# Moving one projection tile, eight transposes and one gate past each other in the rounds of the first attention

## The reference

```python
q, k, v, s = hidden @ Wq, hidden @ Wk, hidden @ Wv, clip(hidden @ Ws, -32, 32)   # per head
z = cumlogsumexp(s, axis=time)
g = exp(concat([z[:1], z[:-1]]) - z);  p = exp(s - z)
hk_t = hk_{t-1} * g_t + k_t (x) p_t;   ok_t = q_t . hk_t         # first pass
pv = softmax(ok)                                                  # over the 64 slots
hv_t = hv_{t-1} * g_t + p_t (x) v_t;   ov_t = pv_t . hv_t        # second pass
o = ov * rsqrt(mean(ov^2) + 1e-5) * g_norm_weight * silu(hidden @ Wg)
x = layernorm(x + o @ Wo)
```

## Time and profile before

| | |
|---|---|
| median of 3 runs | 1235.19 us (1234.74 to 1239.53) |
| profiled execution | 1234.43 us; its span in the trace 1232.5 us |
| PE busy | 949.3 us, 77% of the span |
| DVE busy | 816.3 us, 66% |
| ACT busy | 485.0 us, 39% |
| POOL busy | 385.9 us, 31% |
| mean granted TensorE clock | 0.886 |

### The profile page before, as it was taken

The page is one execution under the profiler, slowest core; times in us unless marked ns, Lnnn a source line. Parts: engine busy times, 40 slices in busy tenths (PEclk is TensorE's granted clock), DMA queues, the critical chain, the costliest instruction groups (busy, mean ns, idle before and its releaser), DMA issues.

```text
span 1232.5 us, 18141 instructions
## 1 busy us (share of the span) xinstructions
PE 949.3 (77%) x5415; PEld 599.4 (49%) x5415; DVE 816.3 (66%) x1474; ACT 485.0 (39%) x823; POOL 385.9 (31%) x325
## 2 busy tenths in 40 slices
PE   6699999999999997448988888830694785888565
PEld 2356556565656555336655556500374443444333
DVE  6568778786878778785544333366677997465766
ACT  3534444534434443302323223204213443777164
POOL 0136472736556464302433333177001000000000
PEclk9699999999999998669999999965697756998787
DMA  4812112111112110220887787733101000000001
GB/s 151 310 56 88 51 55 64 60 55 51 55 52 89 51 43 1 91 71 18 250 254 241 238 260 233 209 95 96 62 1 69 1 1 1 1 0 1 1 1 35
DMA packets 54931, 106.64 MB, mean 87 GB/s; under 512 B 7433, under 2 KB 27537, under 8 KB 54385
## 3 DMA queue, kind: packets, MB, share of 16 engines
q1 hardware_dynamic: 49329, 90.99, 23.1%
q0 software_dynamic: 5568, 15.21, 4.3%
HBM read 86.61 MB, written 19.56 MB: 86 GB/s over the span
## 4 chain that ended last, share of the span: by engine, by line
PE 37%; DVE 27%; SPq 13%; issue 11%; ACT 5%; POOL 4%; DMA 3%; DVEq 0%; ACTq 0%; POOLq 0%
PE ps L617 6%; SPq L519 6%; PE ps L701 3%; PE ps L582 3%; PE ps L572 3%; PE ps L962 3%; DVE row_max L2003 2%; SPq L516 2%; SPq L525 2%; POOL yg L1184 2%; SPq L522 2%; PE ps L630 2%; DVE state L1544 2%; PE ps L1005 1%; PE ps L977 1%
## 5 line engine op out<-in xcount | busy, mean ns | idle before, releaser
L1128 POOL TENSOR_TENSOR state<-state,c_row 128x1024 f32<-128x1024 f32 x32 | 77.4, 2418 | 200.7 <-DVE state L1544 118.1
L617 PE MATMUL ps<-w_vg,xT 128*128 128x512 f32 x256 | 118.0, 604 | 10.2 <-DVE th L1568 10.2
L800 PE MATMUL ps<-w_gv,xgT 128*128 128x352 f32 x272 | 94.5, 480 | 25.3 <-DMA w_gv<-in_w_gv 23.9
L1121 POOL TENSOR_TENSOR drive<-du,b_row 128x1024 f32<-128x1024 f32 x32 | 89.5, 2797 | 55.9 <-DVE y L1694 55.9
L1555 DVE TENSOR_TENSOR aT<-ps,tri 128x768 f32<-128x768 f32 x64 | 59.2, 954 | 42.1 <-PE ps L582 42.1
L572 PE MATMUL ps<-xT,w_qks 128*128 128x512 f32 x192 | 85.0, 593 | 0.3 <-DMA w_qks<-in_wqks 0.3
L1544 DVE TENSOR_TENSOR_SCAN state<-decay,drive 128x1024 f32<-128x1024 f32 x32 | 83.5, 2611 | 0.0
L1168 POOL DMA_INDIRECT xg<-x_dram,tok_cur x68 | 66.6, 979 | 53.6 <-POOL tok_cur L1165 38.6
L2003 DVE TENSOR_REDUCE row_max<-ps 128x1024 f32 x64 | 74.2, 1217 | 7.4 <-PE ps L977 6.6
L617 PEld LDWEIGHTS ps<-w_vg,xT 128*128 128x128 f32 x256 | 46.6, 192 | 65.0 <-issue 45.7
L1801 DVE SCALAR_TENSOR_TENSOR g_th<-g_th,ps 128x176 f32<-128x176 f32 x76 | 25.6, 337 | 78.4 <-ACT g_th L1213 78.3
(11 more groups left out here) (284 smaller groups left out, 2115.3 us busy)
## 6 DMA issues: line engine op xcount, KB each, us to landing
w_gv<-in_w_gv SPq DMA_DIRECT2D x68, 352.0 KB, 4.1
w_dn<-in_w_dn SPq DMA_DIRECT2D x68, 176.0 KB
y_dram<-y_out SPq DMA_DIRECT2D x68, 128.0 KB, 3.5
b_row<-x_dbl_dram SPq DMA_DIRECT2D x16, 512.0 KB, 3.6
c_row<-x_dbl_dram SPq DMA_DIRECT2D x16, 512.0 KB, 4.7
y_dram<-blank SPq DMA_DIRECT2D x2, 3584.0 KB, 22.5
w_vg<-in_wvg SPq DMA_DIRECT2D x8, 512.0 KB, 3.3
w_qks<-in_wqks SPq DMA_DIRECT2D x8, 384.0 KB, 3.0
```

What stands on the lines that cost most here:

```text
L617: last = mm(bank(PJ + t % 2), xT[:, k, t * P:(t + 1) * P], w_vg[:, k, :], start=(k == 0), stop=(k == KD - 1))
L800: last = mm(ps[:, 2 * j + 1, 0:2 * F], x_of(k), w[:, k, :], start=(k == 0), stop=(k == KD - 1))
L1121: G.tensor_tensor(drive[:, n % 2], du[:, e], b_row[:, j], ALU.mult).then_inc(drive_ready, 1)
L1128: G.tensor_tensor(state[:, n % 2], state[:, n % 2], c_row[:, j], ALU.mult).then_inc(read_out, 1)
```

## The change

Three edits, one on each of three engines, in `step` of the first attention:

```diff
@@ PE, step @@
                 last.then_inc(ok_turned, 1)
-                for t in range(4, TILES):
+                for t in range(4, TILES - 1):
                     project_vg(t)
                 pe.wait_ge(slots_exp, at(i, 1, 1))
                 ... 8 transposes of slot_exp, in two halves ...
                     last.then_inc(w_turned, 1)
+                project_vg(TILES - 1)
@@ ACT, step @@
-                for t in range(2, 4):
+                for t in range(2, 5):
                     values_and_gate(t)
                 act.wait_ge(slots_shifted, at(i, 1, 1))
                 f(slot_exp[:], okn[:], ACT.Exp, scale=DK ** -0.5).then_inc(slots_exp, 1)
-                for t in range(4, 6):
-                    values_and_gate(t)
+                values_and_gate(5)
@@ DVE, step @@
-                for t in range(6, TILES):
-                    gate(t)
+                gate(6)
                 for n in range(2):
                     c = slice(n * 512, (n + 1) * 512)
                     dve.wait_ge(w_turned, at(i, 2, n + 1))
                     V.tensor_tensor(wT[:, c], bank(Y + n), zT[:, c], ALU.mult).then_inc(wT_copied, 1)
+                gate(7)
```

## The result

The changed kernel took 1219.64 us (median of 6 runs, 1215.26 to 1220.87) against 1238.55 for the kernel before (6 runs, 1234.74 to 1240.07; three more than stood at the start): a ratio of 0.9846, interval 0.9823 to 0.987. Forecast was 1218.0. Run again later, five times, it gave 1217.59 against 1237.40, ratio 0.9835 (0.9814 to 0.9857). Its profiled execution took 1215.26 us, the span 1213.4, 19.1 less than before.

What follows compares the result with a forecast made beforehand. A round was taken as nearly PE's own work, shortened only where PE waits. 7 x 2.11 + 2.45 = 17.2 us off 1234.43 gives 1217.2, plus 0.76 for the median, stated 1218.0; bounds 1216 to 1220, wider range 1213 to 1225.

Steps and rivals of the forecast that it cites:

- The yardstick: Start of a round's first mask, on which all that follows in the round hangs; claimed 2.11 us earlier.
- Nothing was given back: Stages behind the mask: POOL's 13.36 us idle moves along, ACT keeps 0.94 us before the first square.
- ACT edit: Tile 4's v and tanh ahead of the exponential: costs nothing, and tile 6 starts 1.42 us earlier without a wait.
- PE edit: Transposes ahead of tile 7: no wait, 0.88 us of slot; tile 7's slots end 0.64 us earlier.
- DVE edit: wT ahead of gate(7): eps_sq still waits for POOL's drive, read(0) starts at 242.93, mask at 243.90, 2.11 us earlier.
- two paths: Tile 7 with gate(7), and DVE's own queue, reach the mask 0.1 and 0.2 us from the deciding read(0) path.
- The sum: Seven rounds at 2.11 us plus 2.45 for the first: 17.2 us in all.
- The first round: Round where eps_sq meets no POOL drive, so tile 7 decides: mask at 77.02 instead of 79.47, 2.45 us.
- DVE's queue: Rival: late eps_sq or wT on DVE delays the mask 0.5 to 1.3 us a round; 1222 to 1229, chance 0.11.
- Only one limit: Rival: the mask moves only by tile 7's share, 0.64 us a round, 5 in all; 1230, chance 0.05.
- The clock of the later stages: Rival: from 860 us on, PE's low-clock stretches fall differently and time goes up; 1241 or more, chance 0.04.

## Why the prediction was right

- *The yardstick.* The mask carries the round. It moved by 2.23 us, and the period shrank by 2.23, with 46.93 us behind the mask in both kernels. Nothing was given back: POOL still idles 11.13 us before its next instruction, and ACT's 0.83 us in front of the first square is the 0.94 of the forecast.
- *ACT edit.* Tile 4's activations cost nothing, the exponential was ready as soon as `okn` was, and tile 6 starts without a wait. Undone alone it costs 1.38 us a round; the forecast had tile 6 1.42 earlier.
- *PE edit.* Forecast: transposes without a wait, 0.88 us of slot. Measured 232.00 to 232.87. read(0) was to wait 0.5 us for `wT`; it starts 0.4 behind tile 7's slots (232.87 + 1.72 = 234.59), of which the trace marks 0.23 as idle.
- *DVE edit.* `eps_sq` was forecast to grow to 1.86 us and end with POOL's `drive`: 1.85, and 0.17 in the first round. It was also forecast that this costs only 0.2 us of the round, because two paths end close behind; moving `eps_sq` away gave 0.16.
- *The sum.* 2.11 us a round were forecast, 2.23 came. The term mis-sized is the start of gate(6) and `wT` behind `eps_sq`: I let them follow its end, but gate(6) starts at 233.93, 0.08 ahead of that end, and the first `wT` 4.66 us behind the exponential instead of 4.77. The rows of before had it: a gate behind another instruction, or `wT` behind a gate, starts 0.08 us ahead of the end in front (`wT` at 244.30, the gate before it ends at 244.38). Over 7 rounds that is 0.8 of the 0.9 us between 17.2 and 18.1. The first round gave 2.48 against 2.45. That the stated 1218.0 lies only 1.6 us from the median is in part luck: by medians the gain is 18.9, 1.7 more than forecast, and three more runs of the kernel before had raised its median by 3.4.
- *Rivals.* DVE's queue was to cost a further 0.5 to 1.3 us a round if `eps_sq` waited beyond the end of one `drive`; it did not (1.85 us). The queue does decide the mask, as forecast, but by only 0.14 to 0.16 us. "Only one limit" would have been a mask gain of 0.64, which is what the change gives without its DVE edit (0.66). The clock of the later stages did not shift: 0.81 with the same 262.5 us of PE work. That its falls follow PE's idle stretches is not the whole of it: in the kernel before, it fell at 944 us behind 6 us with 0.70 us of PE work, but also at 981.6 behind 6 us with 5.01. Whole runs of either kernel scatter by some 5 us. The twelve traces show where: up to the first exponential they take 69.6 to 73.9 us, and from the last round's first mask to the end, where nearly the same work is left in all of them, 764.3 to 773.5. Why stays open.

## What to carry to other kernels

Find the one instruction whose start fixes the rest of a repeating stage, list every path that reaches it with its time, and price an edit by the second latest path, not by the wait it removes: 1.68 us of waiting on DVE was worth 0.16, the edits' separate worths sum to 3.46 and gain 2.23. Where stages repeat, measure by the period in the trace, which held to 0.05 us while whole runs scattered by 5. A tiny DVE instruction that takes as long as what is left of a POOL instruction may be a wait for it, as both were here: give it an input in PSUM or a moment when POOL is idle, and ask first what the critical engine does meanwhile.

## What the runs showed of the hardware

A 16-column DVE instruction takes 0.17 us alone and up to 2.25 when it arrives during a POOL instruction of 2.36, here always a `tensor_tensor` from SBUF to SBUF. This held for `scalar_tensor_tensor` with two SBUF inputs and for a one-input f32 `tensor_scalar`, and did not for a `tensor_reduce` from SBUF or for a form with one of its two inputs in PSUM (0.172 us while POOL's `y` ran from 296.41 to 298.76). In the changed kernel each of these 15 instructions (`eps_sq` in seven rounds, `ss` in eight) ended 0.03 us behind the end of POOL's, so their length tells only how early they came. The gate behind `eps_sq` starts 0.08 us before that end.
